# A GRU behind a 16-tap convolution on one core: the order of four small sums in GpSimd's program

## The reference

```
x = x + conv(x, cond_2048)             # y[t] = sum over lag 0..15 of x[t - lag] * tap
def cell(h, x):
    gi = x @ W_ih + b_ih               # 512 x 1536, needs no h
    gh = h @ W_hh + b_hh               # 512 x 1536, needs the step before
    r = sigmoid(i_r + h_r); z = sigmoid(i_z + h_z)
    n = tanh(i_n + r * h_n)
    return (1 - z) * n + z * h
x = x + scan(cell, cond_2048, x)       # 256 steps, everything in float32
```

## Time and profile before

| | |
|---|---|
| time, median of 3 | 988.08 us |
| the profiled execution's own time | 988.25 us |
| its span | 986.4 us |
| TensorE busy, matmuls | 974.2 us (99%) |
| VectorE busy | 881.4 us (89%) |
| ScalarE busy | 514.1 us (52%) |
| GpSimd busy | 558.3 us (57%) |
| granted TensorE clock | 1.00 throughout |

### The profile page before, as it was taken

The page is one execution under the profiler, slowest core; times in us unless marked ns, Lnnn a source line. Parts: engine busy times, 40 slices in busy tenths (PEclk is TensorE's granted clock), DMA queues, the critical chain, the costliest instruction groups (busy, mean ns, idle before and its releaser), DMA issues.

```text
span 986.4 us, 63804 instructions
## 1 busy us (share of the span) xinstructions
PE 974.2 (99%) x26660; PEld 793.8 (80%) x26660; DVE 881.4 (89%) x3075; ACT 514.1 (52%) x2158; POOL 558.3 (57%) x1589
## 2 busy tenths in 40 slices
PE   8999999999999999999999999999999999999997
PEld 5778888888888888888888888888888888888885
DVE  7879999999999999999999999999999988888565
ACT  5334455555555555555555555555555555555543
POOL 4556655556655555555555555655555555555542
PEclk9999999999999999999999999999999999999999
DMA  8731001010010101001010010100101000010000
GB/s 305 68 46 36 24 14 33 20 40 20 16 33 16 41 20 30 24 16 37 20 36 25 13 37 16 41 20 16 37 13 40 15 25 23 12 30 5 25 14 13
DMA packets 67024, 32.43 MB, mean 33 GB/s; under 512 B 44464, under 2 KB 65584, under 8 KB 66736
## 3 DMA queue, kind: packets, MB, share of 16 engines
q1 hardware_dynamic: 66304, 28.25, 11.2%
q10 hardware_dynamic: 432, 0.11, 0.0%
HBM read 19.86 MB, written 8.49 MB: 29 GB/s over the span
## 4 chain that ended last, share of the span: by engine, by line
PE 94%; SPq 3%; DMA 2%; DVE 0%; issue 0%; POOL 0%; ACT 0%; POOLq 0%; DVEq 0%
PE pg L807 66%; PE pcv L612 8%; PE pg L602 8%; PE pg L612 4%; PE pcv L622 4%; PE pcv L632 3%; DMA whh<-w_hh 2%; SPq L309 1%; SPq L303 1%; PE pg L592 1%; DMA xw<-x 0%; PE pcv L602 0%; SPq L334 0%; PE pcv L835 0%; DVE gt L1090 0%
## 5 line engine op out<-in xcount | busy, mean ns | idle before, releaser
L807 PE MATMUL pg<-whh,hp 128*32 128x192 f32 x16368 | 714.8, 327 | 5.0 <-DVE hp L1115 3.6
L807 PEld LDWEIGHTS pg<-whh,hp 128*32 128x32 f32 x16368 | 515.3, 110 | 133.4 <-DVE hp L1115 12.4
L1046 DVE SCALAR_TENSOR_TENSOR pcv<-xb,cnd,pcv 128x256 f32<-128x256 f32 (+2 forms) x588 | 315.0, 536 | 6.9
L998 ACT ACTIVATE rz<-gt 128x64 f32<-128x64 f32 x512 | 136.3, 266 | 293.7 <-DVE gt L1090 267.5
L569 POOL TENSOR_TENSOR nzh<-rz,hp 128x32 f32<-128x32 f32 x512 | 158.2, 309 | 210.7 <-ACT rz L998 209.0
L1090 DVE STREAM_TRANSPOSE gt<-pg 128x128 f32<-128x128 f32 x512 | 161.8, 316 | 50.2 <-PE pg L807 40.8
L1003 ACT ACTIVATE nzh<-an 128x32 f32<-128x32 f32 x512 | 120.9, 236 | 130.7 <-DVE an L1102 130.7
L1115 DVE TENSOR_TENSOR_SCAN hp<-zcp,nzh 128x96 f32<-128x96 f32 x512 | 173.5, 339 | 13.9 <-ACT nzh L1003 9.4
L1102 DVE TENSOR_TENSOR_SCAN an<-rz,gn 128x64 f32<-128x64 f32 x512 | 150.5, 294 | 26.7 <-ACT rz L998 26.7
L1000 ACT ACTIVATE zcp<-gt 128x32 f32<-128x32 f32 x512 | 111.0, 217 | 0.0
L1094 DVE STREAM_TRANSPOSE gn<-pg 128x64 f32<-128x64 f32 x512 | 106.9, 209 | 0.0
(11 more groups left out here) (116 smaller groups left out, 878.3 us busy)
## 6 DMA issues: line engine op xcount, KB each, us to landing
xb<-x SPq DMA_DIRECT2D x96, 94.0 KB, 2.0
out<-x SPq DMA_DIRECT2D x60, 128.0 KB, 1.8
wih<-w_ih SPq DMA_DIRECT2D x4, 768.0 KB, 8.1
whh<-w_hh SPq DMA_DIRECT2D x4, 768.0 KB, 14.6
xw<-x SPq DMA_DIRECT2D x24, 64.0 KB, 3.5
xb<-x SPq DMA_DIRECT2D x16, 62.0 KB, 1.9
tz<-taps SPq DMA_DIRECT2D x12, 64.0 KB, 3.6
xs<-x SPq DMA_DIRECT2D x1, 512.0 KB, 4.4
```

What stands on the lines that cost most here:

```text
L807: i = pe.matmul(pg[t // 2 % Q][f][D * j:D * (j + 1), 0:IN], hp[:, t % 2, 2 * c + 1 - t % 2:2 * c + 3 - t % 2, :, 1].rearrange("p u b -> p ...
L998: act.activation(rz[:, f, :, :, 1].rearrange("p g (c b) -> p (g c) b", b=B), gt[:, f, :, u], ACT.Sigmoid).then_inc(s_rz[f], 1)
L1046: dve.scalar_tensor_tensor(x1_of(c, a, b)[:, lo:hi] if lag == K - 1 else sums, xx[:, c, (K - 1 - lag) * B + lo:(K - 1 - lag) * B + hi], cn ...
```

## The change

In `between(t)`, at r = 0, the two second-level sums are moved ahead of the two first-level ones. Nothing is added or removed.

```
--- before.py
+++ after.py
@@ -519,12 +519,12 @@
                 n = g - FAST + 1
                 seven = e7[:, :] if job(g) else ev[:, 1, IN:]
                 if r == 0:
+                    if job(g + 1):
+                        deep_mixed(g + 1, 1)
+                        deep_mixed(g + 1, 2)
                     if ready(g):
                         mixed(g, 1)
                         mixed(g, 2)
-                    if job(g + 1):
-                        deep_mixed(g + 1, 1)
-                        deep_mixed(g + 1, 2)
                 elif r == 1:
                     if ready(g):
                         mixed(g, 4)
```

## The result

| | before | after |
|---|---|---|
| median of 6 runs | 987.77 us (987.18 to 988.37) | 991.62 us (991.29 to 992.91) |
| profiled execution, its own time | 988.25 us | 991.29 us |
| its span | 986.4 us | 989.6 us |

The ratio is 1.0040, with a 95% interval of 1.0030 to 1.0051: slower by 3.85 us. The forecast was 993.1 with a range of 991.4 to 994.4. The direction and the mechanism came out, the size was too large: +5.0 forecast, +3.85 measured, and 991.62 is only 0.2 above the low end of the range. Of the 1.5 us between forecast and measurement, 0.3 are a difference in the kernel before (988.08 in the three runs known then, 987.77 in all six).

What follows compares the result with a forecast made beforehand. TensorE, 94% of the chain, was taken as the bound. Terms 4.10 + 0.42 + 0.16 + 0.30 + 0.20 - 0.18 = 5.00 us on the profiled 988.25 gave 993.25; less 0.17, 993.1 us, range 991.4 to 994.4.

Steps and rivals of the forecast that it cites:

- The bound: TensorE holds 94% of the chain that ended last; whatever makes its matmuls start later is paid.
- the two kinds of steps: Special steps: 6 where first-level sum L466 waits for the convolution, 7 where second-level sum L491 does; 41 others are ordinary.
- Ordinary steps at zero: At 41 steps of neither kind TensorE's `recur` hides the pair's 0.55 us: 0 to 0.01 us each.
- The chain at step 60: From the convolution's end: L491 start 0.15, pair 0.55, L466 0.40, L470 0.32, L612 0.14; L612 0.82 us later.
- Step 220: Second-kind step where the convolution's instruction is half as long: L612 0.42 us late (0.34 with the short start).
- step 28: Second-kind step where `recur` stands later against the convolution: L612 0.16 us late (0.08 with the short start).
- Contention: On GpSimd, L466 beside VectorE's scan L1102 stretches by 0.04 us (0 to 0.16): 5 x 0.04 = 0.20 us.
- rival 3: The scan holds L466 until it ends, as the skill's rule says: 1.05 us more, 994.1 us; chance 0.10.
- The after-effect of 0.30: Further loss behind a late L612, taken from step 108's 0.06 and added for five second-kind steps: 0.30 us.
- rival 1: The delay is absorbed because VectorE sets the pace behind the late L612: 988.1 to 989 us; chance 0.06.
- The gain of 0.18: At the 6 first-kind steps, earlier L569 and state save 0.03 us each: 0.18 us, at most 0.36.
- second kind: Steps 28, 60, 92, 124, 156, 188, 220, where `deep_mixed` needs front chunks just done: the loss, five at 0.82 us.

Runs made afterwards that it cites:

- experiments 1 and 2: Against the kernel before: changed order at second-kind, first-kind or ordinary steps alone (1.0050, 0.9992, 1.0004); at all 54 steps without the wait (0.9999).
- e_first: Against the kernel before, second-level sums go first only at the 6 steps of the first kind: 986.65 us, ratio 0.9992.
- e_waits: Against the kernel before, the two waits ahead of L466 change places at the 6 steps of the first kind: 988.26 us, ratio 1.0003.
- e_pad: Against the kernel before, a small memset of an unused tile ahead of L466 at the 6 steps of the first kind: 987.71 us, ratio 1.0000.

## Why the prediction was right, and where its size was off

- **The bound, and the two kinds of steps:** right. The cost sits at the seven steps where `deep_mixed` waits for the front chunks, and nowhere else (experiments 1 and 2).
- **Ordinary steps at zero:** right, +0.03 us over 41 steps.
- **The chain at step 60:** 0.15 + 0.55 + 0.40 + 0.32 + 0.14 was forecast and 0.14 + 0.55 + 0.46 + 0.32 + 0.14 came, so L612 was 0.87 late and 0.82 + 0.04 had been said. The higher of the two starts for L491 was the true one: as first behind two waits, it took over L466's 0.14 to 0.15. Step 220 gave 0.42 (0.42 forecast), step 28 0.16 (0.16).
- **Contention:** L466 took 0.38 beside the scan and L470 started 0.06 later, against the 0.04 that was taken. It was not held until the scan's end (255.98), so rival 3 did not happen. The full block that the Trainium skill states (SBUF — State Buffer, Who interferes with whom) is not what this trace shows: it would have put L470 at 255.98 + 0.40 = 256.38 or later, and L470 started at 256.18.
- **The after-effect of 0.30: the step that failed.** "For the 0.06 that come behind the late start I add 5 x 0.06 = 0.30." At steps 60, 124, 156 and 188 the whole delay was 0.89 against a direct 0.87. The 0.06 at step 108 belongs to a step where L612 is late by only 0.27 while the state is late by more, since L569 starts 0.36 behind L612: the next `recur` began 1.18 us behind L612 before (437.13 - 435.95). At step 60 TensorE is later than the state: L569 (256.45) starts 0.19 ahead of L612, and the next `recur` begins 1.14 behind L612 (257.78 - 256.64), as at ordinary steps. At steps 28, 92 and 220 the delay even swallowed waits that were there before: 0.10, 0.06 and 0.05 came back by the next L612. This is rival 1 in small.
- **The gain of 0.18: mis-sized.** It was put at 0 to 0.06 a step, "L470 and L612 stay where they are", and is 0.10 to 0.12. With only the place of the waits changed, 0.43 of the 0.65 is there (0.36 with the memset). What is left, 0.22 to 0.29 in six steps or some 0.04 each, is what comes from the earlier L569 and state: in e_first L569 starts 0.18 ahead of L612 at step 108 and the next `recur` begins 1.14 behind it, where e_waits has 1.17, as before. The profile before had the clue: L466 started 0.15 behind the convolution, and L491 0.07.
- **The sum:** second kind 5.18 forecast, 4.79 measured; gains 0.18 forecast, 0.63 measured. The two errors, 0.39 and 0.45, went the same way, and are the difference between 5.00 and 4.24 but for the 0.08 of the rest. The timed 3.85 (2.96 to 5.04 by its interval) agrees with 4.24.

Why the change lost is the mirror of what it was to bring. It put a pair in front that waits for nothing at six steps, but at seven others it is this pair that waits for the convolution, for data that nobody reads for four steps, and the sums that TensorE needs within the step stand behind it.

## What to carry to other kernels

Before two pieces of an in-order program change places, list for each the steps at which it waits for something late, and look at who is queued behind it there; the average step tells nothing, and here 7 of 54 steps decided. Where a wait for a periodic producer costs anything, moving the producer one step earlier removes the question: it gained 1.9 us, where the best order gained 0.6 in the trace. Look afterwards at what the producer's work now delays: here two steps of six kept most of their loss, one step ahead. And a loss of a few hundredths per step is read from distances between like instructions in two traces, since executions differ by a microsecond at their start.

## What the runs showed of the hardware that was not expected

- A GpSimd instruction that waits for two semaphores starts 0.14 to 0.15 us after the later one if that is the wait listed first (`s_long,s_h1`, convolution last: L466 before, L491 after), and 0.08 us after it if it is the one listed last (`s_h1,s_long` in e_waits, after 1.83 us of idle time against 1.89 before) or the only one (0.08 in e_pad). The order in the listing is the reverse of the order in the program. The packed traces hold the reason, in rows that the views leave out: the wait listed first is an instruction of its own on GpSimd (EVENT_SEMAPHORE), and the one listed last belongs to the sum. At all six steps of the first kind before and all seven of the second after, this instruction starts 0.04 behind the convolution's end and the sum 0.11 behind its start. In e_waits it takes the wait for the state and is over 1.1 us ahead of the convolution's end, and the sum starts 0.08 behind that end.
- A sum on GpSimd and a VectorE scan that overlap delay one another by hundredths, and only when they start close together. The five L466 that started 0.02 to 0.03 behind the scan L1102 (steps 60, 92, 124, 156 and 188 after) took 0.38 in the place of 0.32, and the scan kept its 0.29. At the six steps of the first kind before, L470 started 0.12 to 0.13 ahead of the scan, and it was the scan that grew, to 0.33 to 0.35. But with L470 0.18 to 0.25 ahead, at the eight places after where the two overlap (step 108 among them), neither grew. An estimate from these rows: the scan can't get going before 0.17 behind the sum's start (0.12 + 0.35 - 0.29, or 0.13 + 0.33 - 0.29), and the sum not before 0.08 to 0.09 behind the scan's; the one that comes second doesn't wait for the end of the other.
